# Row maxima prepared by short reductions, a bias stage on GpSimd, and another order of the first loads

## The reference

```python
def _L0_gnn_ref(x, adj, Wq, bq, Wk, bk, Wv, bv, Wo, bo, gamma, beta):    # _L3 is alike, with weights max(adj, 1e-8)
    q, k, v = (proj(Wq, bq), proj(Wk, bk), proj(Wv, bv))                 # 8 heads of 32
    scores = jnp.einsum('bhqd,bhkd->bhqk', q, k) / np.sqrt(D_HEAD)
    mask = adj + jnp.eye(n, dtype=adj.dtype)[None] > 0
    scores = jnp.where(mask[:, None], scores, -jnp.inf)
    attn = jax.nn.softmax(scores, axis=-1)
    out = jnp.einsum('bhqk,bhkd->bhqd', attn, v)
    ...                                                                  # output projection, residual, layer norm

def _L1_gnn_ref(x, adjacency, W_q, b_q, W_k, b_k, W_v, b_v, w_g, b_g):
    ...
    a = x @ w_g[:D]
    c = x @ w_g[D:]
    soul_bias = a[:, :, None] + c[:, None, :] + b_g
    scores = scores + (soul_bias + jnp.log(adjacency + EPS))[:, None, :, :]
    attn = jax.nn.softmax(scores, axis=-1)
    out = jnp.einsum('bhij,bjhd->bihd', attn, V).reshape(B, N, D)
    return out + x
```

## Time and profile before

| | |
|---|---|
| median of 3 runs | 1917.59 us |
| lowest to highest | 1914.16 to 1922.13 us |
| the profiled execution | 1908.63 us |
| its span | 1906.8 us |
| TensorE matmul busy | 1745.8 us (92%) |
| VectorE busy | 1550.6 us (81%) |
| GpSimd busy | 1230.1 us (65%) |
| ScalarE busy | 1216.3 us (64%) |
| mean granted clock of TensorE | 0.981 |

### The profile page before, as it was taken

One profiled execution on the slowest core, in us unless ns is written; L12 is line 12 of the kernel. 1 busy time (PEld: TensorE's weight loads), 2 busy tenths in 40 slices (PEclk: granted clock), 3 DMA queues, 4 the chain that ended last, 5 costly groups with the idle time before them and its releaser, 6 DMA issues.

```text
span 1906.8 us, 54647 instructions
## 1 busy us (share of the span) xinstructions
PE 1745.8 (92%) x23564; PEld 1334.6 (70%) x23564; DVE 1550.6 (81%) x2976; ACT 1216.3 (64%) x1894; POOL 1230.1 (65%) x743
## 2 busy tenths in 40 slices
PE   3899998899999999889999989888999999988996
PEld 2667776677777777577777767667777677766774
DVE  2889887777799988777889988777788998877775
ACT  1567665467777775456877767546777776654675
POOL 2534588368874377728895348754888445883688
PEclk9999999999999999999999999999999999999999
DMA  5110000100221001000111000010021100001001
GB/s 138 40 40 18 13 18 29 41 19 29 63 68 35 13 18 35 17 29 24 51 57 62 24 19 13 30 45 7 19 74 57 51 19 13 18 29 40 13 18 46
DMA packets 67731, 66.44 MB, mean 35 GB/s; under 512 B 6050, under 2 KB 67492, under 8 KB 67492
## 3 DMA queue, kind: packets, MB, share of 16 engines
q1 hardware_dynamic: 67492, 62.95, 11.1%
HBM read 54.54 MB, written 8.39 MB: 33 GB/s over the span
## 4 chain that ended last, share of the span: by engine, by line
PE 74%; DVE 19%; ACT 2%; issue 2%; SPq 1%; POOL 1%; DMA 0%; DVEq 0%; POOLq 0%; ACTq 0%
PE gx L589 22%; PE sc L694 16%; PE od L727 16%; PE gx L740 5%; PE gx L614 3%; PE sc L688 3%; DVE ring L969 3%; PE sc L700 3%; PE gx L776 3%; DVE negm L941 2%; DVE negm L944 2%; DVE qk L923 2%; PE gx L707 2%; DVE lg L1013 1%; DVE negm L957 1%
## 5 line engine op out<-in xcount | busy, mean ns | idle before, releaser
L574 POOL TENSOR_TENSOR ring<-ring,adj_c 128x1024 f32<-128x1024 f32 x256 | 610.4, 2409 | 170.0 <-ACT ring L837 113.0
L694 PE MATMUL sc<-qk 32*128 32x256 f32 x9216 | 417.4, 297 | 11.2 <-ACT m_rows L827 4.4
L694 PEld LDWEIGHTS sc<-qk 32*128 32x128 f32 x9216 | 326.0, 187 | 110.1 <-issue 64.3
L824 ACT ACTIVATE aside<-sc 128x1024 f32<-128x1024 f32 x192 | 196.6, 1024 | 236.1 <-PE sc L694 156.3
L941 DVE TENSOR_REDUCE negm<-sc 128x4 f32<-128x1024 f32 x192 | 234.1, 1219 | 86.2 <-PE sc L694 51.8
L839 ACT ACTIVATE ring<-sc 128x1024 f32<-128x1024 f32 x256 | 248.4, 1023 | 29.8 <-PE sc L700 29.3
L727 PE MATMUL od<-ring,vf 128*32 128x256 f32 x3072 | 243.4, 388 | 3.2 <-POOL ring L574 3.2
L553 POOL TENSOR_TENSOR xs<-xs,bo 128x512 f32<-128x512 f32 x96 | 128.0, 1333 | 182.0 <-DVE xt_lo L915 169.4
L727 PE MATMUL od<-ring,ones_r 128*32 128x256 f32 x3072 | 236.1, 379 | 0.0
L944 DVE TENSOR_REDUCE negm<-aside 128x4 f32<-128x1024 f32 x192 | 232.3, 1210 | 0.0
L579 POOL TENSOR_TENSOR xs<-xs,lr_g 128x512 f32<-128x512 f32 x64 | 86.9, 1357 | 169.8 <-ACT xs L846 169.8
(11 more groups left out here) (141 smaller groups left out, 4320.5 us busy)
## 6 DMA issues: line engine op xcount, KB each, us to landing
adj_c<-in_adj_t SPq DMA_DIRECT2D x96, 256.0 KB, 2.8
adj_r<-in_adj SPq DMA_DIRECT2D x64, 256.0 KB, 2.9
xs<-in_x SPq DMA_DIRECT2D x32, 256.0 KB, 3.1
out<-xs SPq DMA_DIRECT2D x32, 256.0 KB, 2.2
wo<-in_w_o SPq DMA_DIRECT2D x2, 256.0 KB
ring<-in_w_q SPq DMA_DIRECT2D x2, 256.0 KB, 6.5
ring<-in_w_k SPq DMA_DIRECT2D x2, 256.0 KB, 6.7
lr_g<-in_w_bg SPq DMA_DIRECT2D x2, 128.0 KB
```

The source lines that it names most:

```text
L574: pool.tensor_tensor(part, part, adj_c[i.mi % 3][:, t, :].unsqueeze(1).to_broadcast([P, G, N]), ALU.mult).then_inc(weighted, 1)
L694: mm = pe.matmul(sc[:, g, t * N:(t + 1) * N], buf[rows, a, c, t * P:(t + 1) * P], buf[rows, b, c, :], start=(n == 0 and not masked), stop= ...
L824: act.activation(aside[:], sc[:, 0:2, :], ACT.Copy).then_inc(set_aside, 1)
```

## The change

It has two parts.

In U, `tensor_copy`, `tensor_tensor` and `tensor_scalar` are replaced by `tensor_reduce` over axes of length 1, 2 or 3. The maxima now lie in `parts` (layers 0 and 3) or in `negm` beside two more values (layer 1). In layer 1 a reduction of length 3 adds the maximum and what stands beside it, the negated gate and the gate. For every layer a reduction of length 1 with negation rounds, one of length 2 adds the value and the negated high part, and a further one of length 1 writes the high part. M waits for both. The gate and the values beside the maxima are written by a new stage O of GpSimd, in the plan at 3.4 units behind an item's start.

The loads of the first item move to the head of SyncE's queue: x, the adjacency tile, and those parameters that `fold_biases` needs (`fold_plain`, with a semaphore `w_fold` of its own). The weights q, k, v of layer 0 and the two biases are issued from ScalarE's queue. All other parameters and weights come behind the second item's x. Who waited for `w_plain` waits for `w_fold`, or waits later (GpSimd in PC of the second item, VectorE in `extend_fc`).

```diff
 MHA_PLAN1 = {
+    "O": {POOL: [3.4]},
...
+            sp.dma_start(xs[:, 0], x_all[items_l0[0].batch]).then_inc(x_loaded[0], 16)
+            sp.dma_start(adj_r[0][:], adj_all[rows_of[0].batch]).then_inc(adjr_loaded[0], 16)
+            for dst, src in fold_plain:
+                sp.dma_start(dst, src).then_inc(w_fold, 16)
...
-                    if i.k == 0:
-                        for dst, src in first_plain:
-                            sp.dma_start(dst, src).then_inc(w_first, 16)
-                        for n in range(3):
+                    if i.k == 1:
+                        for dst, src in plain:
+                            sp.dma_start(dst, src).then_inc(w_plain, 16)
+                        for n in range(3, len(WEIGHTS)):
                             load_weight(n)
...
+                elif s == "O":
+
+                    a, beside = gate_a[i.i1 % 2], negm[i.i1 % 2][:].rearrange("p (t g) c r -> p t (g c) r", t=T)
+                    pool.wait_ge(v_set, v_count(i))
+                    if i.i1 >= 2:
+                        pool.wait_ge(shifted, i.i1 - 1)
+                    pool.tensor_scalar(a[:], vf[i.mi % NVF][:, :, D], bg_row[:, 0:1], None, ALU.add).then_inc(gate_sum_set, 1)
+                    pool.wait_ge(gate_sum_set, i.i1 + 1)
+                    for t in range(T):
+                        pool.tensor_scalar(beside[:, t, :, 1], a[:, t:t + 1].to_broadcast([P, G * C]), -1.0, None, ALU.mult)
+                    for t in range(T):
+                        last = pool.tensor_copy(beside[:, t, :, 2], a[:, t:t + 1].to_broadcast([P, G * C]))
+                    last.then_inc(gate_set, 1)
...
-                    pe.wait_ge(negp_set, i.mi + 1)
+                    pe.wait_ge(negp_set, 2 * i.mi + 2)
...
                     if i.l == 1:
-                        a = gate_a[i.i1 % 2]
-                        dve.wait_ge(v_set, v_count(i))
-                        dve.tensor_scalar(a[:], vf[i.mi % NVF][:, :, D], bg_row[:, 0:1], None, ALU.add).then_inc(gate_set, 1)
                         dve.wait_ge(gate_set, i.i1 + 1)
-                        for t in range(T):
-                            dve.tensor_scalar(neg[:, :, t, :], neg[:, :, t, :], a[:, t:t + 1], a[:, t:t + 1], ALU.subtract, ALU.add)\
-                                .then_inc(shifted, 1)
-                        dve.wait_ge(shifted, T * i.i1 + T)
-                    dve.tensor_copy(pad[:, :, :, :, 0], neg[:]).then_inc(neg_hi_set, 1)
+                        dve.tensor_reduce(value, negm[i.i1 % 2][:], AX_X, ALU.add).then_inc(shifted, 1)
+                        dve.wait_ge(shifted, i.i1 + 1)
+
+                    dve.tensor_reduce(both[:, :, :, 0], value.unsqueeze(3), AX_X, ALU.max, negate=True).then_inc(neg_hi_set, 1)
                     dve.wait_ge(neg_hi_set, i.mi + 1)
-                    dve.tensor_tensor(pad[:, :, :, :, 1], neg[:], pad[:, :, :, :, 0].bitcast(F32), ALU.subtract).then_inc(negp_set, 1)
+                    with nc.allow_low_precision(reason="the difference fits"):
+                        dve.tensor_reduce(pad[:, :, 1:2 * C:2], both[:].bitcast(F32), AX_X, ALU.add).then_inc(negp_set, 1)
+                    dve.tensor_reduce(pad[:, :, 0:2 * C:2], both[:, :, :, 0:1].bitcast(F32), AX_X, ALU.max, negate=True).then_inc(negp_set, 1)
```

More of the change, by code:

```diff
@@ L260, in gnn_stack @@
     for engine in (PE, ACTE, DVE, POOL):
-        for group in ("T", "QP", "V", "S", "U", "M", "E", "A", "N", "F", "H", "B", "Z", "Y", "G", "J", "K", "L", "X", "W", "C", "XB", "PR", "PC"):
+        for group in ("T", "QP", "V", "S", "U", "M", "E", "A", "N", "F", "H", "B", "Z", "Y", "G", "J", "K", "L", "X", "W", "C", "XB", "PR", "PC", "O"):
             stages = (group,) if len(group) > 1 and group != "QP" else tuple(group)
@@ L466, in _ @@
                     sp.dma_start(adj_r[i.ar % 3][:], adj_all[i.batch]).then_inc(adjr_loaded[i.ar % 3], 16)
-                    if i.k == 0:
-                        for dst, src in plain:
-                            sp.dma_start(dst, src).then_inc(w_plain, 16)
-                        for n in range(3, len(WEIGHTS)):
-                            load_weight(n)
                 elif s == "LC":
@@ L523, in _ @@
             pool.tensor_scalar(b_col["q0"][:], b_col["q0"][:], SCALE, None, ALU.mult).then_inc(cols_set, 1)
-            pool.wait_ge(w_plain, 16 * len(plain))
-            for name in ("q1", "q3"):
-                pool.tensor_scalar(b_col[name][:], b_col[name][:], SCALE, None, ALU.mult).then_inc(cols_set, 1)
             def diagonal(buf):
@@ L555, in _ @@
                 elif s == "PC":
+                    if i.k == 1:
+                        pool.wait_ge(w_plain, 16 * len(plain))
+                        for name in ("q1", "q3"):
+                            pool.tensor_scalar(b_col[name][:], b_col[name][:], SCALE, None, ALU.mult).then_inc(cols_set, 1)
                     buf = adj_c[i.mi % 3]
@@ L789, in split @@
                                scale=SCALE if name[0] == "q" else 1.0).then_inc(w_hi_set, 1)
+            for n in range(3):
+                if n == 1:
+                    for dst, src in first_plain:
+                        act.dma_start(dst, src).then_inc(w_first, 16)
+                name = WEIGHTS[n]
+                act.dma_start(staged[name][:, :, 0:D], w[name].rearrange("(c p) e -> p c e", p=P)).then_inc(w_raw[n], 16)
             split(0)
```

38 lines of the change are left out of this document (24 added, 14 removed).

## The result

| | before | after |
|---|---|---|
| median | 1918.07 us (4 runs) | 1840.28 us (4 runs) |
| lowest to highest | 1914.16 to 1922.13 | 1840.06 to 1841.73 |
| profiled execution | 1908.63 | 1840.3 |
| its span | 1906.8 | 1838.4 |
| mean granted clock | 0.981 | 0.990 |

The ratio is 0.9596, with a 95% interval from 0.9575 to 0.9616. The two profiled executions differ by 68.3 us, the forecast of the sum was 68. The medians differ by 77.8 us, because the unprofiled runs before scatter and all lie above their profiled one, while those after stay within 2 us.

The account below looks back on a forecast made before the run. The prediction took U, held on VectorE while GpSimd multiplies, and the start to bound the kernel. U's two places give 48 us and the start 20, together 68, so 1849 us was forecast, with a range of 1832 to 1875.

Parts of the forecast that it names:

- What bounds the kernel: TensorE's M waits eight times for H behind U, 35.1 us, and 29.6 us for the first transpose; other waits short.
- U without the stall: Short reductions in U are not held; layer 1 saves 11 us of VectorE, layers 0 and 3 add 10; counted nothing.
- the rival sum of 38 us: By the skill's rule on slow reductions, the 64 longer U's cost 10 us in full: 38 instead of 48.
- The second place: Around 313 us, once per group: 6.1 us idle before M plus 2.6 us clock; 7.5 of 8.7 us taken.
- what is late next: At the second place GpSimd can begin the item's multiplications only 5.5 us earlier, not 8.7; TensorE has other stages until then.
- The first place: Around 267 us, once per group: 3.3 us idle before M and Q plus 1.5 us clock; 4.8 us, 4.5 taken.
- the other long U's: Long U's whose delay no TensorE wait shows leave VectorE earlier; some more gain in the upper bound of 58 us.
- O: New GpSimd stage, some 1.1 us an item, 35 us in all, hidden in idle time; counted 0, at most 35 us.
- The start: Loads issued earlier bring the first Q at 8 to 10 us; 20 us gain taken, ends 14 and 24.
- from there the program goes on as before: After the copy of the first scores, at 25.2 instead of 44.84, everything continues unchanged, 20 us earlier.
- The rival that the loads crowd: The start gives 10 us instead of 20, so 1859 us; chance 0.12.
- The other rivals: Clock stays low: 1872, chance 0.14; stall moves to GpSimd's multiplications: 1886, chance 0.07; reductions held too: 1972, chance 0.02.

Follow-up runs that it names:

- no_mult: Kernel before, with GpSimd's multiplications by the weights in layers 1 and 3 on only 8 columns of one head; 1834.21 us.
- copies: Changed kernel, with U's high part written by tensor_copy and the difference by tensor_tensor, as before; 1872.49 us, ratio 0.9769.
- gate_on_dve: Changed kernel, with layer 1's gate kept on VectorE by tensor_scalar and no stage O; the split keeps its reductions; 1876.86 us, ratio 0.9805.
- start_only: Changed kernel with the new order of loads, but U and the gate as before; 1894.43 us, ratio 0.9884.
- halves: Kernel before, with each of GpSimd's multiplications by the weights cut into two instructions over half the heads; 1916.61 us, ratio 0.9999.
- weights_first: Changed kernel, with four weights (q, k, v of layer 1 and one of layer 2) issued ahead of the small parameters; 1836.45 us, ratio 0.9579.

## Why the prediction held, and where it did not

- **What bounds the kernel** was read rightly: U held by GpSimd, and the start. But "outside the start its waits are short, with one exception" passed over the wait for L923, 25.5 us, third in the list: eight of its eighteen, 18.7 us, stand behind VectorE's multiplications of layer 0 that GpSimd holds: four of 1.4 us, which shrank to 0.4 with the change, and four of 3.3, which stay. `no_mult` shows the cause, `copies` and `gate_on_dve` the kinds of operation. That the stall gives way to reductions followed from the earlier trace rows, and all four lines of U stayed below 0.21 us (limit given: 0.3).
- **U without the stall.** The estimates of 210, 177, 194 and 177 ns were 191, 164, 186 and 160. The longer U of layers 0 and 3 cost nothing that shows: the rival sum of 38 us, by the rule on reductions, is out, since U and O together gave 53 to 56, of which 4.6 are the XB that O holds back.
- **The second place:** 6.1 + 2.6 computed, 7.5 taken; 6.2 us at M and up to 2.2 for the clock came, then 1.8 went back. The step "what is late next" had the right engine and the right size, 5.5 us for GpSimd against 5.4 measured, but the wrong consequence: TensorE did not wait for a multiplication. VectorE had come further forward than GpSimd, and so L1048 of layer 2 ran into its pair. 6.4 a group instead of 7.5, four times: -4.
- **The first place:** 4.5 taken, 5.0 measured: +2. I had discounted the computed 4.8 without a reason from a row.
- **Not in the sum:** 4.6 us at the first items of layer 1, 3.2 behind them and 2.0 at early items, 10 us in all. Only the last 2.0 are "the other long U's", which I had named in the upper bound. The 4.6 are the XB that O moved out of VectorE's way, and no term or rival of the prediction has that. The 3.2 are shorter stretches at low clock; `start_only` has 1.7 of them too, with all its U's held, so they are not U's alone.
- **O:** 0 counted, and no cost shows (the doubled O is 1.6 us slower, within the scatter). But where O waits for V it holds back XB, and that gains the 4.6 us.
- **The start:** 20 forecast, 15.5 measured in this pair, in the range of 14 to 24 near its lower end (up to 18.9 against the other profiles with the old loads). The first Q started at 7.41 us (8 to 10.4 forecast; the terms of the latter add up to 10.2). Two terms failed. One is the landing of `in_w_q1`: 9.5 us, where I took 5.7 from the earlier trace rows and 7.6 at most. The issue was even 1.2 us earlier than computed, behind six tiles of 256 KB and not four, and the first scores were set aside 17.6 us earlier. The other is "from there the program goes on as before": 2 more us were lost up to M. VectorE begins to reduce those scores at 29.30 us, 2.0 behind ScalarE's copy, where both began at 44.84 before; until then it makes low parts of the late weights and folds biases. The low clock from 24 to 32 us (0.53 and 0.61, after TensorE had been idle for 8.03 us) does not carry the loss, since TensorE waits for VectorE at 38.53 again, 4.40 us against 4.64 at the same step before. The rival that the loads crowd had the mechanism of the first term and too high a price: 10 us, where the late landing took 2 to 3.
- **The tail** costs 2.6 us in this pair, and was not in the sum: the last item now has two windows at low clock ahead of it, 0.50 from 1820 to 1824 us and 0.69 from 1824 to 1828, and before the span's last such stretch began only near 1900. Why is open: `halves` has such a tail with U as before.

```profile
1820.00:1824.00 4.00, 2.98 (x22) 0.50 0.00 0
1824.00:1828.00 4.00, 4.00 (x14) 0.69 0.39 131
```

- **The sum.** 15.5 + 4 x 5.0 + 4 x 6.4 + 10 - 2.6 is 68.5, forecast 68. It was right by errors that cancel, so in part by luck: start -4.5, second place -4, tail -2.6, and +2 and +10 on the other side. The start lay in its own range (14 to 24) and U with O in theirs (36 to 58, 55.5 measured); the tail was in none. The median came 9 us lower than 1849: the offset of 9 us between the median and the profiled run of before, which I carried over, vanished with the change. Part of the offset can be placed: against the other profiles with the old loads, that profiled run is about 2 us early at its first M, and its tail is 2.2 us shorter than that of `halves`. Where the rest comes from I can't say. Nor can I say whether the held steps cause the scatter; `halves` scatters as before does, `no_mult` doesn't, but neither does `start_only`, which has all the holds.
- **The other rivals** are out: no low clock at either place, no reduction held, and TensorE's waits for L594 stayed at 3.1 us.

## What to carry over

A small step whose median is 0.2 us and whose maximum is 2.3 waits for something: look at what the neighbour engine's long instruction does at that moment, and for an operation in the same trace, on the same memory, that never stretches. When a stall goes, work out for each engine how far its next instructions come forward. They don't move alike (here 8.3 us on VectorE and 5.4 on GpSimd), and steps meet that did not meet before; here it was one step of another layer. An instruction that waits also moves what stands behind it in its queue: O held XB back, and that alone gained 4.6 us. A long wait of TensorE for a VectorE step can be a hold of the instruction before that step, so the list of waits needs a look at durations too. And of loads at the start, the ones that the program needs first should be issued first, each with a semaphore of its own: moving one weight forward is worth only the distance to the next thing that waits for everything.

## What I had not expected of the hardware

- Cutting GpSimd's instruction in two gives nothing to a chain of short VectorE steps: each step waits for a border of its own, 1.2 us instead of 2.3, and more steps are caught.
- A held copy can pass borders: 6.64 us over four of them, and 0.6 us past the end of GpSimd's run, once in 96.
- Loads of rows spread over 128 partitions, a few bytes or 1 KB each, kept the DMA engines busy at 80 GB/s (share 0.66), while weights moved at 320 GB/s (share 1.01) just before; behind them the weight landed 9.5 us after its issue, and ahead of them, in `weights_first`, 5.7.
- Moving two kinds of tiny steps from VectorE to GpSimd made them no cheaper (0.2 to 0.3 us each there, five an item), yet it paid: on VectorE they are held, up to 2.38 us, on GpSimd they stood in idle time.
